# Turning the feed-forward rows by DVE blocks and copies inside SBUF, in place of TensorE, for the middle batches

## What is computed

```
x = x + 0.5 * ffn(layernorm(x))
x = x + attn(layernorm(x))
x = x + 0.5 * ffn(layernorm(x))

ffn(x):  h = layernorm(x) * ln_gamma + ln_beta
         y = silu(h @ w1 + fc1_bias)          # 128 -> 512
         return x + 0.5 * (y @ w2 + fc2_bias) # 512 -> 128
attn(x): q, k, v for 16 heads of 8 features
         a = relu(q k^T / sqrt(8));  a = a / (sum(a) + 1e-6)
         y = x + (a v) @ w_out + b_out
         return layernorm(y) * gamma + beta
```

## Time and profile before

| | |
|---|---|
| median of 3 runs | 365.14 us (364.57 to 365.54) |
| the profiled execution, its own time | 364.41 us |
| its span | 362.3 us |
| PE busy | 352.5 us, 97% |
| DVE busy | 264.0 us, 73% |
| ACT busy | 228.3 us, 63% |
| POOL busy | 210.3 us, 58% |
| granted TensorE clock, mean | 1.000 of full speed |

### The profile page before, as it was taken

One profiled execution on the slowest core, in us unless ns is written; L12 is line 12 of the kernel. 1 busy time (PEld: TensorE's weight loads), 2 busy tenths in 40 slices (PEclk: granted clock), 3 DMA queues, 4 the chain that ended last, 5 costly groups with the idle time before them and its releaser, 6 DMA issues.

```text
span 362.3 us, 12675 instructions
## 1 busy us (share of the span) xinstructions
PE 352.5 (97%) x5002; PEld 159.5 (44%) x5002; DVE 264.0 (73%) x659; ACT 228.3 (63%) x419; POOL 210.3 (58%) x445
## 2 busy tenths in 40 slices
PE   8989999998999999999999999999999999999996
PEld 6733423442335533364335533355234643532364
DVE  4666576876787975879676985879758785678773
ACT  3377577576766477755777377764777466578623
POOL 7595237359753898148853599248881582236541
PEclk9999999999999999999999999999999999999999
DMA  7017016300541027100350016200270004500001
GB/s 215 6 29 179 3 28 156 80 3 2 116 119 33 2 61 183 52 4 31 91 146 31 4 40 161 69 28 2 71 186 11 3 31 111 124 31 4 0 4 60
DMA packets 14105, 22.70 MB, mean 63 GB/s; under 512 B 2528, under 2 KB 3808, under 8 KB 14048
## 3 DMA queue, kind: packets, MB, share of 16 engines
q1 hardware_dynamic: 11456, 17.83, 20.0%
q10 hardware_dynamic: 2592, 4.07, 3.4%
HBM read 3.54 MB, written 2.10 MB: 16 GB/s over the span
## 4 chain that ended last, share of the span: by engine, by line
PE 84%; POOL 5%; DVE 5%; ACT 2%; issue 2%; DMA 1%; POOLq 0%; ACTq 0%; DVEq 0%
PE o_bank L734 30%; PE scores L711 14%; PE pre_bank L655 10%; PE pre_bank L648 9%; PE post_bank L648 9%; PE post_bank L655 5%; PE scores L655 3%; PE pre_bank L641 2%; DVE probs L1284 1%; ACT probs L1017 1%; POOL norm_x_rs L1317 1%; PE post_bank L641 1%; DMA pre_x<-in_x_dram 1%; PE o_bank L635 1%; POOL u L1345 1%
## 5 line engine op out<-in xcount | busy, mean ns | idle before, releaser
L1284 DVE TENSOR_SCALAR probs<-scores 128x512 f32<-128x512 f32 x235 | 150.6, 678 | 62.6 <-PE scores L711 60.6
L1017 ACT ACTIVATE probs<-scores 128x512 f32<-128x512 f32 x264 | 142.2, 596 | 57.3 <-PE scores L711 55.6
L734 PE MATMUL o_bank<-probs,v_op 128*32 128x512 f32 x1024 | 135.5, 601 | 1.0 <-ACT probs L1017 0.4
L711 PE MATMUL scores<-q_op,k_op 32*128 32x512 f32 x499 | 69.2, 495 | 0.5 <-DVE q_op L1221 0.4
L711 PEld LDWEIGHTS scores<-q_op,k_op 32*128 32x128 f32 x499 | 27.5, 181 | 80.7 <-issue 59.7
L734 PEld LDWEIGHTS o_bank<-probs,v_op 128*32 128x32 f32 x1024 | 23.3, 108 | 35.8 <-issue 35.2
L910 ACT ACTIVATE pre_y<-pre_bank,b_sum,col_consts 128x512 f32<-128x512 f32 x28 | 21.8, 778 | 22.6 <-PE pre_bank L655 22.6
L648 PEld LDWEIGHTS post_bank<-w,post_y 128*32 128x32 f32 x960 | 26.6, 110 | 11.8 <-issue 11.3
L648 PE MATMUL post_bank<-w,post_y 128*32 128x128 f32 x960 | 31.1, 273 | 0.0
L648 PE MATMUL pre_bank<-w,pre_y 128*32 128x128 f32 x960 | 29.9, 273 | 0.0
L648 PEld LDWEIGHTS pre_bank<-w,pre_y 128*32 128x32 f32 x960 | 26.2, 110 | 7.9 <-issue 5.5
(11 more groups left out here) (173 smaller groups left out, 442.9 us busy)
## 6 DMA issues: line engine op xcount, KB each, us to landing
k_op<-k_parts SPq DMA_DIRECT2D x62, 128.0 KB, 2.7
q_op<-q_parts SPq DMA_DIRECT2D x62, 128.0 KB, 2.7
out_dram<-o_rows ACTq DMA_DIRECT2D x7, 256.0 KB, 2.0
pre_x<-in_x_dram ACTq DMA_DIRECT2D x6, 256.0 KB, 2.6
w_int<-in_L_ffn_fc_q_dram SPq DMA_DIRECT2D x2, 256.0 KB, 3.8
rows<-in_lines_dram ACTq DMA_DIRECT2D x1, 256.0 KB, 5.9
s_rows<-in_L_ffn_fc_scales_dram SPq DMA_DIRECT2D x1, 256.0 KB, 6.3
wqk<-in_w_qk_dram SPq DMA_DIRECT2D x1, 256.0 KB, 6.5
```

Source lines behind the costliest of these rows:

```text
L711: mm(score_bank(b, s, i, j), k_op[rows, g, P * kt:P * (kt + 1)], q_op[rows, g, :], start=True, stop=True).then_inc(scores_done[i], 1)
L734: last = mm(o_bank[pair][VW * j:VW * (j + 1), :], v_op[:, kt, heads_of(g).start + 2 * j, :], probs[:, s % 2, j, :], start=(odd == 0 and kt ...
L1017: activation(probs[:, s % 2, 2 * i + j, :], score_bank(b, s, i, j), ACT.Relu).then_inc(probs_done[i][j], 1)
L1284: v.tensor_scalar(probs[:, s % 2, 2 * i + j, :], score_bank(b, s, i, j), 0.0, None, ALU.max).then_inc(probs_done[i][j], 1)
```

## The change

The rows of pre for batches 2 to 7 (`PRE_BY_DMA`) and of post for batches 1 to 5 (`POST_BY_DMA`) aren't turned by PE any more. A new task `turn` on DVE turns the 16 blocks of 32x32 of each 128x128 tile from h into a new tile `blocks`; then SP copies the blocks to their places in t with 16 DMAs inside SBUF, 32 partitions of 512 bytes each. The columns of t are then ordered by quarters of the partitions, and the second layer reads its tokens in that order (`by_quarter`). The task hT of these batches is gone on PE and ACT, and the counters of fills are worked out for each batch. The first layer waits for the copies; the next rows may be written once DVE has read the old ones. SP issues the copies of a turn ahead of the copies of k and q of the same batch.

The tables are rewritten: fc1.0 of the next but one batch takes the place of pre.hT, so pre's first layer runs one step earlier; post.fc1.0 starts one step later; in batches 2 to 6 oT.0 and den.0 move from step 8 to 10, a.0 from 10 to 13, x_stats from 10 to 14; POOL makes the pre rows at the front of a batch; batch 1 gets an order of POOL's of its own; and x is loaded for one batch further ahead.

```diff
+TURN_DONE = 16 * HG * HG
+PRE_BY_DMA, POST_BY_DMA = range(2, B), range(1, B - 2)
...
 PE_ORDER = [
...
-    (["pre.uT@1", "post.hT@-1"], []),
...
+    (["pre.uT@1"], []),
...
-    (["post.fc1.3@-1"], ["pre.hT@2"]),
+    (["post.fc1.3@-1"], ["pre.fc1.0@2"]),
...
 DVE_ORDER = [
...
+    ["pre.turn@2"],
...
+    ["post.turn@-1"],
...
             def __init__(self, n, fills, by_dma, buffers):
+                self.blocks = sb(f"{n}_blocks", [P, HG, P])
+                self.turned, self.t_in = sem(f"{n}_turned"), sem(f"{n}_t_in")
...
+            def rows_read(self, b):
+                return (self.turned, self.turns(b)) if b in self.by_dma else (self.full, self.after("hT", b))
...
+            def turn(st, b):
+                sp.wait_ge(st.turned, st.turns(b))
+                if b > 0:
+                    sp.wait_ge(st.full, st.after("fc1.3", b - 1))
+                for i in range(HG):
+                    for j in range(HG):
+                        sp.dma_start(st.t[VW * j:VW * (j + 1), P * i:P * (i + 1)], st.blocks[VW * i:VW * (i + 1), j, :]
+                                     ).then_inc(st.t_in, 16)
+
             def iteration(b):
-                n, per = b + 1, len(PRE_FILLS)
+                n = b + 1
+                if n > 0 and b + 2 in pre.by_dma:
+                    turn(pre, b + 2)
+                if b - 1 in post.by_dma:
+                    turn(post, b - 1)
                 for g in range(NG):
...
-            def by_tokens(into, tokens, t, w, start, stop):
+            def by_tokens(into, tokens, t, w, start, stop, by_quarter=False):
 
                 for j in range(HG):
-                    part = slice(P * t + VW * j, P * t + VW * (j + 1))
+                    first = P * j + VW * t if by_quarter else P * t + VW * j
+                    part = slice(first, first + VW)
...
-                    else:
-                        next_fill(st, b, what)
+                    elif free_before(st, b, what) > 0:
+                        pe.wait_ge(st.free, free_before(st, b, what))
+                    if f == 0 and b in st.by_dma:
+
+                        pe.wait_ge(st.t_in, TURN_DONE * st.turns(b))
+                        if st is post:
+                            pe.wait_ge(y_done, b + 1)
                     by_columns(into, w1_whole[:, cols], st.t[:, :]).then_inc(st.full, 1)
...
+                elif what == "turn":
+                    st = pre if stage == "pre" else post
+                    dve.wait_ge(st.rows, b + 1)
+                    if st.turns(b) > 1:
+                        dve.wait_ge(st.t_in, TURN_DONE * (st.turns(b) - 1))
+                    v.transpose(st.blocks[:, :, :].rearrange("p j (t c) -> p t j c", t=TT),
+                                st.h[:, :, :].rearrange("p t (j c) -> p t j c", c=VW)).then_inc(st.turned, 1)
...
-                            pool.wait_ge(pre.full, len(PRE_FILLS) * (b - 1) + pre.n("hT"))
+                            pool.wait_ge(*pre.rows_read(b - 1))
```

More of the change, by code:

```diff
@@ L184 @@
     [],
[L185 to L190, removed]
+    ["post.store@-2", "pre.uT@1"],
+    ["pre.k@1"],
+    ["pre.q@1", "post.fc1.0@-1"],
+    ["post.fc1.1@-1"],
+    ["pre.v@1", "post.fc1.2@-1"],
+    ["post.fc1.3@-1", "pre.fc1.0@2"],
 ]
@@ L225 @@
     [],
-    ["pre.x1@1"],
+    ["pre.turn@2", "pre.x1@1"],
     ["pre.x1_stats@1"],
@@ L258 @@
     ["post.y@-1", "post.y_stats@-1"],
-    [],
+    ["pre.turn@2"],
     [],
@@ L608, in iteration @@
                     elif g == 0:
-                        sp.wait_ge(pre.free, per * n + pre.n("k"))
+                        sp.wait_ge(pre.free, pre.after("k", n))
                     for i in range(2):
@@ L614, in iteration @@
                     elif g == 0:
-                        sp.wait_ge(pre.free, per * n + pre.n("q"))
+                        sp.wait_ge(pre.free, pre.after("q", n))
                     for i in range(2):
@@ L748, in task @@
                     elif what == "v":
-                        pe.wait_ge(pre.free, per * b + pre.n("uT"))
+                        pe.wait_ge(pre.free, pre.after("uT", b))
                         next_fill(pre, b, "v")
@@ L1104, in task @@
                     elif what == "x1":
-                        dve.wait_ge(pre.full, per * b + pre.n("fc2"))
+                        dve.wait_ge(pre.full, pre.after("fc2", b))
                         dve.wait_ge(pre.res, b + 1)
@@ L1112, in task @@
                     elif what == "x1_stats":
-                        dve.wait_ge(pre.free, per * b + pre.n("fc2"))
+                        dve.wait_ge(pre.free, pre.after("fc2", b))
                         row_stats(norm_x1, b, x1)
@@ L1143, in task @@
                     elif what == "out":
-                        dve.wait_ge(post.full, per * b + post.n("fc2"))
+                        dve.wait_ge(post.full, post.after("fc2", b))
                         dve.wait_ge(post.res, b + 1)
@@ L1401, in task @@
                     else:
-                        pool.wait_ge(pre.free, len(PRE_FILLS) * b + pre.n("v"))
+                        pool.wait_ge(pre.free, pre.after("v", b))
                     if b > 0:
@@ L1477, in _ @@
             for b in range(1, B):
-                for beside in POOL_ORDER:
-                    work(b, beside)
+                work(b, POOL_SECOND if b == 1 else POOL_ORDER)
             work(B, POOL_LAST)
```

194 lines of the change are left out of this document (93 added, 101 removed).

## The result

The changed kernel takes **383.26 us** (median of 4 runs, 381.69 to 384.14) against 365.09 us (364.57 to 365.54) of the kernel before, run beside it: a ratio of 1.0495, 95% interval 1.0463 to 1.0527, so 18 us slower. The prediction said 364.1 us, range 360.5 to 369.0; it was wrong, and what happened is its rival 1. The profiled execution took 381.69 us, the shortest of the four, with a span of 379.7 us where before had 362.3: 17.4 us to account for. The other three took 1.4 to 2.5 us more and have no profile; what they lost there isn't shown.

The account below looks back on a forecast made before the run. PE was taken as the bound, busy 97% of the span. Turns removed (-6.19), den's collision gone (-0.88) and two new waits (+3.0, +3.0) sum to -1.07 us, giving 364.1 us, range 360.5 to 369.0.

Parts of the forecast that it names:

- rival 1: Post copies land late, at 0.63 us each; PE stands 2.4 to 3.1 us in five batches: 376 to 380 us, chance 0.20.
- the price of a copy: SP's issue of each 16 KB copy inside SBUF, taken as 0.38 us; lateness decides from about 0.42 to 0.47.
- The turns removed from PE: Six pre turns of 0.59 us and five post turns of 0.53 go from PE's path: 6.19 us off.
- Den in batch 1: Den's small addition on DVE no longer collides with a POOL addition in batch 1: 0.88 us gained.
- fc1.2 to fc1.3: In step 15 of batches 1 to 6 fc1.3 waits for ACT to empty the post bank: 6 x 0.5 = 3.0 us back.
- k to q: In step 12 of batches 2 to 6 q waits for DVE to take k's low part: 5 x 0.6 = 3.0 us back.
- The meeting of den with POOL: Den, now in step 10, meets POOL's post residual; half a POOL instruction is counted in q's wait, 1.0 us in all.
- DVE costed at nothing: DVE's added turns, 1.4 us per middle batch against 9.8 us idle, were taken to cost nothing.
- rival 3: DVE becomes the bound, all eleven turns on the path, scores waiting in steps 4 and 9: 371.9 us, chance 0.05.
- Rival 2: The two new waits on PE aren't there: 361.1 us with one wait less, 358.1 with none, chance 0.13.

Follow-up runs that it names:

- run 3: The changed kernel, but the 16 copies per turn read pieces of the same shape from the input in HBM, not DVE's blocks in SBUF: 366.58 us in one run.
- run 1: Against the kernel before, only the pre rows of batches 2 to 7 are turned by DVE and copies; PE still turns the post rows: 361.22 us, ratio 0.9904.
- run 5: As run 4, but post.fc1.2 and v change places on PE and ACT in batches 1 to 6: 359.98 us, ratio 0.9873 to the kernel before.
- run 4: The changed kernel, but each turn goes through HBM by 5 transfers, one store and 4 loads: 362.67 us, ratio 0.9945 to the kernel before.
- run 7: The changed kernel, but ACT issues the last six of each post turn's 16 copies and SP ten: 369.90 us in one run.

## Why the prediction was wrong

**The step that failed** is the price of a copy: "I take 0.38, since the copies of k cut a row of their source in two, and these don't." The runs showed 0.59 us of issue and 0.63 from one to the next. For copies inside SBUF the shape made no difference: 32 rows (16 KB), 128 rows (64 KB) and k's 128 KB all take 0.6. The row I chose differs in two other things. ACT's load reads HBM, where k's copies stay inside SBUF: from HBM the same 16 copies have 0.46 from one to the next (run 3), so 0.17 of the missing 0.25 is the memory. And ACT's load stands alone: in run 3 the first copy of a turn takes 0.31 us and those behind it 0.42, a difference about as large as the rest. The row that is nearest in place, and not in form, had the answer; by it rival 1 was the likeliest case, and not one of 0.20.

**Rival 1** has the mechanism right in each number: the turn is done 2.62 us after step 8 (step 8 starts at 120.72, the turn ends at 123.34), and PE goes on 14.6 after step 8 in batch 2 (14.0 to 14.7 worked out). What it left out is the clock; with those 3.2 us its 376 to 380 become 379 to 383. On the Trainium skill's rule that transfers under 64 KB are mostly overhead (page "DMA: Bandwidth & Descriptors", Rules for kernel authors): the trace agrees. Four transfers of 64 KB cost a quarter of sixteen of 16 KB, and took 20 us off the kernel.

**The turns removed from PE**: 0.60 us per batch measured for pre (run 1) against 0.59. Post gives 0.44, as step 10 shrinks to 2.02 and not to 1.93.

**Den in batch 1**: 0.22 us, and batch 1's step 2 is back at 3.18 in the changed kernel. Right.

**fc1.2 to fc1.3**: step 15 at 3.68 (3.65 forecast), a wait of 0.53 against 0.5. Right; run 5 takes it away.

**k to q**: 0.30 against 0.6, half of what I took. Probs start 1.09 us after step 11 (1.23 forecast) and k's low part ends 2.97 after it (3.14); PE wants the bank at 2.73, as forecast. The meeting of den with POOL didn't come: den took 0.21.

**DVE costed at nothing**: right; steps 4 and 9, where **rival 3** would have shown, last 2.51 and 2.30 in the changed kernel. **Rival 2** fell too, as both waits are there, 0.53 and 0.30.

Without the late copies the sum was near: with the orders unchanged and the turns in time, run 4 comes out 1.9 us under the kernel before, where -1.07 was forecast. Of the difference, 1.5 is the smaller q wait, against it 0.45 the smaller gain in step 10 and 0.2 the longer wait in step 15.

What stays open is why a copy within SBUF takes longer to issue than a load (0.33 to 0.43) or a store (0.34): each of these has one end in SBUF, and only with both ends there is it 0.59.

## What to carry to other kernels

Count DMA instructions before bytes: the queue that issues them works one after another, and the price of one is to be read from a row with the same source and destination memory, however different its shape, and from copies that follow one another if yours do. When two rows give prices on both sides of the point from which a rival decides, that rival is the forecast's equal. A transfer that pays per instruction may go faster by a longer way with fewer instructions.

## What the runs showed of the hardware

- Issue: 0.59 to 0.60 us per copy inside SBUF, on SP at 16, 64 and 128 KB and on ACT at 16; on SP 0.42 for 16 KB from HBM, 0.31 for the first of a turn; 0.34 for a store of 256 KB. With both queues issuing copies (run 7), SP's ten took 7.1 us on average (6.7 to 7.5); the first ten of the change's sixteen, issued by SP alone, took 6.6 (6.2 to 7.2).
- In run 7 ACT issued a copy (123.38, 0.61 us) while it computed (123.32, 0.60), but the copy of k behind two issues of 1.25 and 0.87 us stood 1.33 us.
- PE's granted clock fell to the 1.2 GHz level behind 2 of 5 stands of 2.3 to 3.4 us (the change), in all 5 of 7.4 to 8.5 us with eight more copies (in batch 2 it was at 0.50 while PE still stood), and once behind 1.40 us (run 7). A wait may thus cost more than its length: 1.6 us behind a stand of 3.0.
